# Query normalisation read by ScalarE from the projection's bank, output projection written to the attention output's bank, and weights split in thirds, in a post-norm decoder layer

## The chip, the cores and the metric

The kernel runs on one core of one Trainium2 chip. The metric is the device time of one execution in microseconds (us). Three runs of the kernel before gave 2011.68 us as their median (2011.28 to 2014.92).

## What is computed

A decoder layer on `x` of 4 sequences x 512 rows x 512 columns, in three parts, each followed by a residual sum and a layer norm:

```
x = _layernorm(x + attn(x, Wq, Wk, Wv, Wo))        # attention over the 512 channels
x = _layernorm(x + xattn(x, ctx, ...))             # the part that is changed
x = _layernorm(x + ffn(x, w_gate_up, w_down))      # ternary weights, int8-like activations
```

The middle part, cut to what matters (16 query heads of width 128 in 8 groups, two heads a group; a second set of 16 query heads looks at a context of 64 rows):

```
q  = _ln(fp8_linear(ln_out, wq))     # per head of 128 columns: subtract mean, times rsqrt(var + EPS)
qx = _ln(fp8_linear(ln_out, wqx))
k  = _ln(fp8_linear(ln_out, wk));  v = fp8_linear(ln_out, wv)
kx, vx = split(cond @ w_kv_x);     kx = _ln(kx)
core = softmax(q k^T / sqrt(128)) v;   xout = softmax(qx kx^T / sqrt(128)) vx
out  = round_to_fp8(concat(core, xout) / smooth) @ wproj * scale
```

## The kernel before

**Stages.** Stage A is the first attention, all in fp32. Stage B is the middle part, and the only one whose code changes. Stage C is the feed-forward part. Each engine has its own instruction list, written out by hand, and the engines meet only at counting semaphores: a wait on one engine holds everything that stands behind it on that engine. So the order of the work is exactly the order of the code; there is no planner.

**Loops of stage B.** The outer loop is over 8 groups `g`, the inner one over 4 sequences `b`. One such (g, b) is called a *pair* here, with the number n = 4g + b, 32 in all. A pair has 4 steps `st`, each for 128 rows of queries; a step has the number T = 4n + st. While step `st` of pair n does attention, the engines also project the queries, keys and values of pair n + 1, a tile of 128 rows at a time.

**PSUM banks.** There are 8 banks of 128 x 512 fp32. `S0`, `S1` take the scores of the two heads, `T0`, `T1` the transposed probabilities, `OB` the attention output (columns 0:256 own attention, 256:512 context), `P0` the query projection *and* the output projection, `P1` keys and values, `MB` transposed queries and keys and the context scores.

**A step on TensorE**: two score products (L496), the key/value projection (`proj_kv`) and the query projection (`proj_q`, both through `project`, L391), the attention output `av` of the step before (L446 own, L452 context), the transposes of the probabilities (L530), of the normalised queries (`turn_q`, L425) and, once a pair, of the keys (`turn_k`, L431), and the output projection of two steps before (`project_out`, L458). Step 0 also has the context scores (L567), and in every second pair the context's keys and values (L419); step 1 has the transposes of the context probabilities (L502).

**The path of the queries.** `proj_q` fills `P0`; ScalarE copies it whole to `raw` in SBUF (`raw_kv`, recorded at L662, where all plain copies are) and, behind it, keys and values to `KV`; VectorE takes mean and variance of the four heads from `raw` (`head_stats`, L1017 to L1031); GpSimd computes the inverse deviations in two operations (`deviations`, L1305 and L1307); VectorE normalises keys (`head_norm`, L1039) and the four heads of queries (L1041) into `nq`; TensorE transposes them and ScalarE copies them out with the gain (`qt_out`, L733; `kt_out`, L739, for keys). `P0` is free for the next product as soon as `raw` is written. `turn_k` is the last transposing of a step 3, in the same bank `MB` as `turn_q` just ahead of it, so it waits for `qt_out`.

**The path of the scores.** VectorE takes the row maximum (L1094), ScalarE the exponential with its row sum (L786), VectorE scales the row (`scale_rows`, L1049 and L1051), TensorE transposes, ScalarE copies to `prT` (L662).

**The output.** ScalarE copies `OB` out with the smoothing scale (`ob_out`, L774), VectorE rounds to fp8 in five operations (`round_terms`, L1057 to L1067), TensorE multiplies by `wp` into `P0`, VectorE adds it to `x1` (`accumulate`, L1071). In step T VectorE rounds the terms of T - 1 after it has scaled the rows of T.

**Weights.** A group's four projection matrices arrive in one DMA of 1.5 MB (`load_proj`). Each weight is kept as a sum of two fp16 numbers: ScalarE makes the high part (`split_high`, L700), VectorE the low part (`split_low`, L1010). `wst`, `wh` and `wl` have one buffer each, so the new group's parts are made in the pairs b = 2 and b = 3, after the last use of the old ones and just ahead of the first use of the new ones, which is in step 0 of b = 3.

Of the kernel before, what the change touches and what calls it, by code (L numbers as in the profile page):

```python
# [25 lines left out]
P = 128  # L26
# [15 lines left out]
WCOL = {Q: (0, 256), QX: (256, 512), K: (512, 640), V: (640, 768)}  # L42
NW = 768
# [20 lines left out]
def build(nc, a, out):  # L64
    ctx = ExitStack()
    with ctx:
# [3 lines left out]
        def sb(stack, name, shape, dt=F32):  # L70
# [40 lines left out]
        rdev = sb(ctx, "rdev", [P, 7])  # L111
        mv = sb(ctx, "mv", [P, ST, 2])
# [27 lines left out]
        wst = sb(stB, "wst", [P, KT, NW])  # L140
        wh = sb(stB, "wh", [P, KT, NW], F16)
        wl = sb(stB, "wl", [P, KT, NW], F16)
# [4 lines left out]
        raw = sb(stB, "raw", [P, D])  # L147
# [49 lines left out]
            wst_loaded wkx_loaded wpst_loaded  # L197
# [7 lines left out]
            max_ready exp_done raw_out kv_out kvx_out qt_out kt_out kxt_out ob_out pt_out pxt_out xexp_done  # L205
# [7 lines left out]
        out_stored = [sem(f"out_stored{i}") for i in range(2)]  # L213
        xt_loaded = [sem(f"xt_loaded{i}") for i in range(2)]
# [4 lines left out]
        def tern(c):  # L219
            if c < 8:  # L220
                return wgu[:, c // 2, (c % 2) * F:(c % 2 + 1) * F]
            return wdn[:, (c - 8) * 4:(c - 7) * 4, :].rearrange("p k n -> p (k n)")

# [5 lines left out]
        def _(sp):  # L229
# [21 lines left out]
            def load_proj(g):  # L251
                if g:
                    sp.wait_ge(s["wl_ready"], 4 * g)
                sp.dma_start(wst[:], a["wcat"][g].rearrange("(k p) n -> p k n", p=P)).then_inc(s["wst_loaded"], 16)
# [27 lines left out]
            load_proj(0)  # L282
            load_context(0)
            load_out(0)
# [3 lines left out]
            load_proj(1)  # L288
            for n in range(TT):
# [7 lines left out]
                if b == 3 and g + 2 < NG:  # L297
                    load_proj(g + 2)
                if n + 1 < TT:
                    load_abs(n + 1)  # L300

# [27 lines left out]
        def _(pe):  # L329
# [57 lines left out]
            def project(dst, c, j, b):  # L387
                lo, hi = WCOL[c]
                for k in range(KT):
                    for m, w in enumerate((wh, wl)):  # L390
                        ins = mm(dst, XQ[:, c, k, b * S + j * P:b * S + (j + 1) * P], w[:, k, lo:hi],  # L391
                                 start=(k == 0 and m == 0), stop=(k == KT - 1 and m == 1))
                return ins

            def proj_q(n, j, b, weights=None):
                for c in (Q, QX):
                    lo, hi = WCOL[c]
                    if weights is not None:
                        pe.wait_ge(s["wl_ready"], weights + (3 if c == Q else 4))
                    ins = project(P0[:, lo:hi], c, j, b)  # L400
                ins.then_inc(s["proj_q_made"], 1)

            def proj_kv(n, part, b, weights=None):
                if 3 * n + part:
                    pe.wait_ge(s["kv_out"], 3 * n + part)
                if weights is not None:
                    pe.wait_ge(s["wl_ready"], weights + 2)
                if part == 0:
                    pe.wait_ge(s["kvx_out"], n // 2 + 1)
                    if n >= 2:  # L410
                        pe.wait_ge(s["kxt_out"], (n - 1) // 2 + 1)
                for i, j in enumerate(KVPART[part]):
                    for c, lo in ((K, 0), (V, P)):
                        ins = project(P1[:, 256 * i + lo:256 * i + lo + P], c, j, b)
# [13 lines left out]
            def turn_k(n):  # L428
                pe.wait_ge(s["nq_ready"], 4 * n + 3)
# [4 lines left out]
            def turn_kx(n):  # L434
                pe.wait_ge(s["ident_set"], 2)
                pe.wait_ge(s["nq_ready"], 4 * n + 1)
# [3 lines left out]
            def av(T):  # L440
                n, st = T // ST, T % ST
                pe.wait_ge(s["pt_out"], 2 * T + 2)
                if T:
                    pe.wait_ge(s["ob_out"], T)
                for t in range(ST):
                    mm(OB[:, 0:2 * P], KV[:, n % 2, t, P:2 * P], prT[:, st % 2, t, :, :].rearrange("p h s -> p (h s)"),  # L446
                       start=(t == 0), stop=(t == ST - 1))
                if st == 0:
# [19 lines left out]
            pe.wait_ge(s["wl_ready"], 4)  # L468
            for j in range(4):
                if j:  # L470
                    pe.wait_ge(s["raw_out"], j)
                if j < 3:
                    proj_kv(0, j, 0)
                proj_q(0, j, 0)
# [8 lines left out]
            def pair(g, b, first, last):  # L483
                n = 4 * g + b
                nxt = not (last and b == 3)
                for st in range(ST):
                    T = 4 * n + st
                    if st == 0:
                        pe.wait_ge(s["kt_out"], n + 1)
                        pe.wait_ge(s["qt_out"], 4 * n + 3)  # L490
                    for h in range(2):
                        if T:
                            pe.wait_ge(s["exp_done"], 2 * T + (h - 1))
                        if st == 3 and h == 0:
                            pe.wait_ge(s["qt_out"], 4 * n + 4)
# [8 lines left out]

                    def next_proj():
                        if T >= 3:
                            pe.wait_ge(s["acc_done"], T - 2)
                        if st < 3:
                            proj_kv(n + 1, st, (b + 1) % 4)
                        pe.wait_ge(s["raw_out"], 4 * n + 4 + st)  # L510
                        proj_q(n + 1, st, (b + 1) % 4)

                    if nxt and st in (1, 3):
                        next_proj()
                    if T:
                        av(T - 1)
                    if nxt and st == 2:
                        next_proj()
                    if st == 0 and T >= 2:
                        pe.wait_ge(s["acc_done"], T - 2)  # L520
                        pe.wait_ge(s["raw_out"], 4 * n + 4)
                        project_out(T - 2)
                    for h in range(2):
# [8 lines left out]
                        if h == 0 and st == 0:  # L532
                            pe.wait_ge(s["kt_out"], n + 1)
                            turn_q(n, 3)
                        if h == 0 and st and nxt:
# [871 lines left out]
```

## Time and profile before

| | |
|---|---|
| median of three runs | 2011.68 us |
| the profiled execution, its own time | 2012.47 us |
| its span, first to last instruction | 2010.7 us |
| TensorE busy | 1809.7 us (90%) |
| VectorE busy | 1535.9 us (76%) |
| ScalarE busy | 1064.5 us (53%) |
| GpSimd busy | 263.1 us (13%) |
| mean granted TensorE clock | 0.972 of full |
| chain that ended last | PE 71%, DVE 16%, ACT 9%, issue 3%, POOL 1% |

In the profile PE is TensorE, DVE VectorE, ACT ScalarE, POOL GpSimd, SP the engine that issues DMAs. Busy time of PE goes to the modelled end of its pipelined matmuls, so two matmuls in a row overlap in the records; what a group of matmuls takes of the engine is best read as the distance from its start to the start of the next group. The pairs of stage B lie between 425.6 us and some 1764 us of the span; the start of each pair is seen by the copy of its transposed keys (L739), of which there are 32.

### The profile page before, as it was taken

The numbers are of one execution on the slowest core, as the hardware profiler recorded it, in microseconds if no ns is written. First come the engines' busy times: TensorE is split into PE (matmuls) and PEld (weight loads), VectorE is DVE, ScalarE is ACT, GpSimd is POOL, SyncE is SP. The second block draws the span as 40 slices with busy tenths as digits, with TensorE's granted clock in tenths as the row PEclk, the third lists the DMA queues.
The fourth block names the chain that finished last, engine by engine and source line by source line (L and its number), as shares of the span: only waits on it lengthen the run. The fifth ranks groups of instructions, "written<-read, shape, count | busy, mean of one in ns | idle before, by whom it ended". The sixth has DMA issues, their size and how long they took to land.

```text
span 2010.7 us, 32238 instructions
## 1 busy us (share of the span) xinstructions
PE 1809.7 (90%) x11024; PEld 1248.2 (62%) x11024; DVE 1535.9 (76%) x4964; ACT 1064.5 (53%) x2526; POOL 263.1 (13%) x361
## 2 busy tenths in 40 slices
PE   8999999459999999989999999998999999839897
PEld 3444444337767777777777777777777777614443
DVE  0175754778887888788888788888888888788997
ACT  1121111226666666666666666666666666565555
POOL 0000000011211211111121121111211112011110
PEclk9999999769999999999999999999999999969999
DMA  5000000210011011001101101100110000420000
GB/s 210 21 0 22 0 0 0 75 61 20 17 42 41 10 42 37 21 10 41 42 17 42 42 9 42 37 21 11 39 42 17 10 10 9 176 84 16 22 22 27
DMA packets 37761, 70.78 MB, mean 35 GB/s; under 512 B 3296, under 2 KB 14048, under 8 KB 36576
## 3 DMA queue, kind: packets, MB, share of 16 engines
q1 hardware_dynamic: 37600, 68.73, 10.0%
q8 instruction: 90, 1.47, 0.3%
q14 instruction: 71, 0.58, 0.1%
HBM read 63.47 MB, written 4.19 MB: 34 GB/s over the span
## 4 chain that ended last, share of the span: by engine, by line
PE 71%; DVE 16%; ACT 9%; issue 3%; POOL 1%; DMA 0%; ACTq 0%; POOLq 0%; DVEq 0%; SPq 0%
PE bank L335 17%; PE bank L391 14%; PE bank L446 10%; PE bank L496 10%; PE bank L458 5%; PE bank L530 4%; PE bank L452 3%; PE bank L567 2%; DVE wl L1010 2%; ACT yb L774 2%; PE bank L425 2%; DVE am L1195 2%; ACT qT L733 2%; ACT hb L862 1%; ACT wh L700 1%
## 5 line engine op out<-in xcount | busy, mean ns | idle before, releaser
L391 PE MATMUL bank<-wh,XQ 128*128 128x256 f16 (+1 forms) x2048 | 355.8, 249 | 25.2 <-DVE wl L1010 24.0
L391 PE MATMUL bank<-wl,XQ 128*128 128x256 f16 (+1 forms) x2048 | 359.9, 249 | 0.0
L786 ACT ACTIVATE pr<-bank,nmx 128x512 f32<-128x512 f32 x256 | 175.8, 691 | 178.2 <-DVE nmx L1094 174.5
L496 PE MATMUL bank<-kT,qT 128*128 128x512 f32 x512 | 250.9, 613 | 0.8 <-ACT kT L739 0.7
L446 PE MATMUL bank<-prT,KV 128*128 128x256 f32 x1024 | 242.3, 379 | 0.5 <-ACT prT L662 0.4
L391 PEld LDWEIGHTS bank<-wh,XQ 128*128 128x128 bf16 x2048 | 204.0, 100 | 49.1 <-DVE wl L1010 20.1
L446 PEld LDWEIGHTS bank<-prT,KV 128*128 128x128 f32 x1024 | 189.5, 190 | 52.5 <-issue 23.0
L391 PEld LDWEIGHTS bank<-wl,XQ 128*128 128x128 bf16 x2048 | 202.9, 99 | 22.8 <-issue 10.3
L1307 POOL TENSOR_TENSOR rdev<-gvar,cst 128x7 f32<-128x7 f32 x128 | 190.5, 1488 | 10.0
L1094 DVE TENSOR_REDUCE nmx<-bank 128x1 f32<-128x512 f32 x256 | 169.5, 684 | 25.4 <-PE bank L496 22.1
L774 ACT ACTIVATE yb<-bank,rsT 128x128 bf16<-128x128 f32 x512 | 146.6, 372 | 79.0 <-PE bank L452 79.0
L1305 POOL TENSOR_TENSOR gvar<-mvB,geps 128x7 f32<-128x7 f32 x128 | 27.3, 213 | 1126.2 <-DVE mvB L1031 1126.2
L662 ACT ACTIVATE prT<-bank 128x512 f32<-128x512 f32 x256 | 157.5, 616 | 7.5 <-PE bank L530 7.5
L530 PE MATMUL bank<-identf,pr 128*128 128x128 f32 x1024 | 154.4, 274 | 6.3 <-DVE pr L1051 6.2
L662 ACT ACTIVATE raw<-bank 128x512 f32<-128x512 f32 x128 | 76.3, 596 | 154.4 <-PE bank L391 81.4
L496 PEld LDWEIGHTS bank<-kT,qT 128*128 128x128 f32 x512 | 95.0, 196 | 90.5 <-issue 64.3
L1041 DVE TENSOR_SCALAR nq<-raw,mvB,rdev 128x128 f32<-128x128 f32 x512 | 142.2, 342 | 0.7 <-POOL rdev L1307 0.7
L458 PE MATMUL bank<-wp,cq 128*128 128x512 bf16 x512 | 132.2, 381 | 2.9 <-DVE x L1071 2.9
L733 ACT ACTIVATE qT<-bank,hlq 128x256 f32<-128x256 f32 x256 | 132.7, 584 | 1.2 <-PE bank L425 1.1
L1051 DVE TENSOR_SCALAR pr<-pr,ri 128x512 f32<-128x512 f32 x256 | 124.6, 487 | 9.1
L530 PEld LDWEIGHTS bank<-identf,pr 128*128 128x128 f32 x1024 | 121.6, 142 | 14.7 <-DVE pr L1051 8.3
L614 PE MATMUL bank<-wgu,xiT 128*128 128x512 bf16 x512 | 118.5, 387 | 10.3 <-ACT hs L856 6.9
(157 smaller groups left out, 3032.0 us busy)
## 6 DMA issues: line engine op xcount, KB each, us to landing
wst<-in_wcat SPq DMA_DIRECT2D x8, 1536.0 KB, 6.8
wpst<-in_wproj SPq DMA_DIRECT2D x8, 1024.0 KB, 5.2
wa<-in_wgu SPq DMA_DIRECT2D x32, 256.0 KB, 2.6
wch<-in_wgu SPq DMA_DIRECT2D x8, 1024.0 KB, 12.1
xT<-in_xT SPq DMA_DIRECT2D x4, 1024.0 KB, 5.4
x<-in_x SPq DMA_DIRECT2D x4, 1024.0 KB, 11.9
wkx<-in_wkvx SPq DMA_DIRECT2D x8, 512.0 KB, 4.1
wa<-in_wdn SPq DMA_DIRECT2D x32, 128.0 KB, 2.6
```

Source lines behind the costliest of these rows:

```text
L335: ins = mm(dst, lhs(k), rhs(k), start=(k == 0), stop=(k == n - 1))
L391: ins = mm(dst, XQ[:, c, k, b * S + j * P:b * S + (j + 1) * P], w[:, k, lo:hi], start=(k == 0 and m == 0), stop=(k == KT - 1 and m == 1))
L446: mm(OB[:, 0:2 * P], KV[:, n % 2, t, P:2 * P], prT[:, st % 2, t, :, :].rearrange("p h s -> p (h s)"), start=(t == 0), stop=(t == ST - 1))
L458: ins = mm(P0[:, :], cq[:, T % 2, c * P:(c + 1) * P], wp[:, c, :], start=(c == 0), stop=(c == 3))
L496: mm(SB_[h][:], qT[:, h, st * P:(st + 1) * P], kT[:, :], start=True, stop=True).then_inc(s["scores_made"], 1)
L530: ins = nc.tensor.transpose(TB_[h][:, t * P:(t + 1) * P], pr[:, h, t * P:(t + 1) * P], identf[:])
L662: return act_f(dst, src, ACT.Copy)
L733: ins = act_f(qT[:, 2 * c:2 * c + 2, j * P:(j + 1) * P], MB[:, c * 256:(c + 1) * 256].rearrange("p (h s) -> p h s", h=2), ACT.Identity, sc ...
L774: ins = act_f(yb[:, T % 2, c * P:(c + 1) * P], OB[:, c * P:(c + 1) * P], ACT.Copy, scale=rsT[:, T // 16, c:c + 1])
L786: act_f(pr[:, h, :], SB_[h][:], ACT.Exp, bias=nmx[:, st, h:h + 1], accum_out=su[:, st, h:h + 1]).then_inc(s["exp_done"], 1)
L1094: v.tensor_reduce(nmx[:, st, h:h + 1], SB_[h][:], AX.X, ALU.max, negate=True).then_inc(s["max_ready"], 1)
L1307: g.tensor_tensor(rdev[:], gvar[:], CPOW, ALU.pow).then_inc(s["stats_ready"], 1)
```

## The change

Five things change, all in stage B.

1. **Queries.** `raw` and the copy into it are gone. VectorE's `head_stats` reads `P0` itself. GpSimd's `deviations` has two operations more: the negated means (`nmean`) and their product with the inverse deviations (`nbias`). ScalarE's new `q_norm` writes `nq` straight from `P0` in four activations of 128 x 128 (scale `rdev`, bias `nbias`); it stands at the head of the next step, ahead of the exponentials. VectorE's `head_norm` keeps only the keys, as `k_norm`. TensorE's next `proj_q` waits for `nq_ready`.
2. **Output projection.** It goes to `OB` instead of `P0`: it waits for `ob_out` of the step before, and `av` waits for the `accumulate` before it.
3. **Order.** TensorE: `av_context` is apart from `av` and, in step 1, behind `proj_q`; `turn_k` in step 3 stands ahead of the transposes of the probabilities, and `turn_q(n + 1, 2)` at the end of the step; `project_out` stands at the same place in all steps. VectorE: `round_terms(T - 2)` between the maxima and `scale_rows`, where `round_terms(T - 1)` stood behind; one `accumulate` at the head of each step; `head_stats(n + 1, 0)` ahead of the row sums of the context probabilities. ScalarE follows.
4. **Weights.** They come in thirds of 512 KB (queries; context queries; keys and values) through two slots of `wst`. The query weights have two buffers (`whq`, `wlq`), the key and value weights one. Each third is split in two halves, by ScalarE at the end of steps 2 and 3, by VectorE at the end of step 3 and in step 0 of the next pair, in the pairs b = 0, 1, 2.
5. **DMA queue.** `load_proj` now follows `load_abs` in pairs b = 0, 1, 2, and waits for the split of the third that used the slot.

```diff
-            def raw_kv(n, j, par):
-                act.wait_ge(s["proj_q_made"], 4 * n + j + 1)
-                    act.wait_ge(s["nq_ready"], 4 * n + j)
-                copy(raw[:, :], P0[:, :]).then_inc(s["raw_out"], 1)
+            def q_norm(n, j):
+                act.wait_ge(s["stats_ready"], 4 * n + j + 1)
+                for h in range(4):
+                    ins = act_f(nq[:, j % 2, h * P:(h + 1) * P], P0[:, h * P:(h + 1) * P], ACT.Identity,
+                                scale=rdev[:, h:h + 1], bias=nbias[:, h:h + 1])
+                ins.then_inc(s["nq_ready"], 1)
...
             def head_stats(n, j, par):
-                dve.wait_ge(s["raw_out"], 4 * n + j + 1)
+                dve.wait_ge(s["proj_q_made"], 4 * n + j + 1)
                 for h in range(4):
-                    v.bn_stats(bnB[:, h, :], raw[:, h * P:(h + 1) * P])
+                    v.bn_stats(bnB[:, h, :], P0[:, h * P:(h + 1) * P])
...
-                for h in range(4):
-                    ins = v.tensor_scalar(nq[:, j % 2, h * P:(h + 1) * P], raw[:, h * P:(h + 1) * P], mvB[:, h, 0:1], rdev[:, h:h + 1],
-                                          ALU.subtract, ALU.mult)
-                ins.then_inc(s["nq_ready"], 1)
...
                 own.do(g.tensor_tensor(gvar[:], mvB[:, :, 1], geps[:], ALU.add))
-                own.sync()
-                g.tensor_tensor(rdev[:], gvar[:], CPOW, ALU.pow).then_inc(s["stats_ready"], 1)
+                own.do(g.tensor_tensor(nmean[:], mvB[:, 0:4, 0], cst[:, 5, 0:4], ALU.mult))
+                own.sync()
+                if tile:
+                    pool.wait_ge(s["nq_ready"], tile)
+                own.do(g.tensor_tensor(rdev[:], gvar[:], CPOW, ALU.pow))
+                own.sync()
+                g.tensor_tensor(nbias[:], nmean[:], rdev[:, 0:4], ALU.mult).then_inc(s["stats_ready"], 1)
...
             def project_out(T):
                 pe.wait_ge(s["cq_ready"], T + 1)
+                pe.wait_ge(s["ob_out"], min(T + 2, 4 * TT))
                 for c in range(4):
-                    ins = mm(P0[:, :], cq[:, T % 2, c * P:(c + 1) * P], wp[:, c, :], start=(c == 0), stop=(c == 3))
+                    ins = mm(OB[:, :], cq[:, T % 2, c * P:(c + 1) * P], wp[:, c, :], start=(c == 0), stop=(c == 3))
```

TensorE, a step, after the two score products:

```diff
+                    if nxt and st in (1, 2):
+                        proj_kv(n + 1, st)
...
                     if T:
                         av(T - 1)
+                    if nxt and st == 1:
+                        proj_q(n + 1, st)
+                    if T:
+                        av_context(T - 1)
+                    if nxt and st > 1:
+                        proj_q(n + 1, st)
...
+                    if nxt and st == 3:
+                        pe.wait_ge(s["qt_out"], 4 * n + 4 + 2)
+                        turn_k(n + 1)
...
-                        if h == 1 and st == 3 and nxt:
-                            pe.wait_ge(s["qt_out"], 4 * n + 4 + 3)
-                            turn_k(n + 1)
...
                         project_out(T - 2)
+                    if st == 3 and nxt:
+                        pe.wait_ge(s["kt_out"], n + 2)
+                        turn_q(n + 1, 2)
```

VectorE, a step, after the two maxima:

```diff
+                    if T >= 2:
+                        round_terms(T - 2)
+                    if nxt and st:
+                        k_norm(n + 1, st - 1, (b + 1) % 2)
+                    scale_rows(T, st)
+                    if nxt and st:
+                        head_stats(n + 1, st, (b + 1) % 2)
+                    if b < 3 and not last and st == 3:
+                        split_low(3 * (g + 1) + b, 0)
                     if st == 0:
-                    if T:
-                        round_terms(T - 1)
+                        if b and not last:
+                            split_low(3 * (g + 1) + b - 1, 1)
```

## Rows read from the trace of the kernel before

**Rows 1.** Stretches of pairs b = 0 to 3: stretch, length, busy and records by engine, clock, DMA.
```profile
599.20:639.20 40.00, 38.27 (x282) 30.20 (x280) 33.17 (x117) 26.34 (x67) 6.86 (x8) 1.00 0.11 37
639.20:680.30 41.10, 39.77 (x291) 31.86 (x290) 33.55 (x120) 25.51 (x67) 6.74 (x8) 1.00 0.07 25
680.30:721.20 40.90, 38.23 (x282) 30.22 (x281) 33.16 (x117) 26.68 (x71) 6.87 (x8) 1.00 0.04 11
721.20:766.90 45.70, 41.70 (x291) 32.52 (x290) 38.85 (x136) 28.52 (x75) 7.09 (x9) 0.96 0.14 46
```

**Rows 2.** Waits of PE from 440 to 1720 us: total, times, longest.
```profile
PE bank L431 <- ACT qT L733: 46.4, 30, 2.3
PE bank L391 <- DVE wl L1010: 18.7, 21, 1.8
```

**Rows 3.** Timeline of ACT: starts of pairs n = 1 and n = 31.
```profile
471.37 0.78 ACT L739 ACTIVATE kT<-bank,hln 128x512 f32<-128x512 f32 x1 [0.26 <-PE bank L431]
...
1723.49 0.78 ACT L739 ACTIVATE kT<-bank,hln 128x512 f32<-128x512 f32 x1 [0.26 <-PE bank L431]
```

**Rows 4.** Timeline of PE from a step 3 (b = 1) on: start, length, what, idle before.
```profile
1004.90 1.88 PE L496 MATMUL bank<-kT,qT 128*128 128x512 f32 x4
1006.61 0.27 PE L391 MATMUL bank<-wh,XQ 128*128 128x256 f16 x1
...
1008.36 1.89 PE L446 MATMUL bank<-prT,KV 128*128 128x256 f32 x8
...
1010.53 0.60 PE L530 MATMUL bank<-identf,pr 128*128 128x128 f32 x4
1010.97 0.60 PE L425 MATMUL bank<-identf,nq 128*128 128x128 f32 x4
...
1013.33 0.66 PE L431 MATMUL bank<-identf,kn 128*128 128x128 f32 x4 [1.32 <-ACT qT L733]
1013.82 1.03 PE L458 MATMUL bank<-wp,cq 128*128 128x512 bf16 x4
1014.86 1.98 PE L496 MATMUL bank<-kT,qT 128*128 128x512 f32 x4
...
1027.76 0.66 PE L502 MATMUL bank<-identf,px 128*128 128x128 f32 x4 [0.39 <-DVE px L1125]
```

**Rows 5.** Timeline of DVE around the same place, in steps 3 and 0.
```profile
1009.89 0.86 DVE L1017 BATCH_NORM_STATS2 bnB<-raw 128x6 f32<-128x128 f32 x4
...
1017.49 1.11 DVE L1041 TENSOR_SCALAR nq<-raw,mvB,rdev 128x128 f32<-128x128 f32 x4
1018.51 0.16 DVE L1049 RECIPROCAL ri<-su 128x1 f32<-128x1 f32 x1
...
1020.22 0.29 DVE L1057 TENSOR_SCALAR yb<-yb 128x512 bf16<-128x512 bf16 x1 [0.44 <-ACT yb L774]
...
1022.01 0.75 DVE L1071 SCALAR_TENSOR_TENSOR x<-bank,pscale,x 128x512 f32<-128x512 f32 x1
```

**Rows 6.** Timeline of POOL, the same tile.
```profile
1011.25 0.20 POOL L1305 TENSOR_TENSOR gvar<-mvB,geps 128x7 f32<-128x7 f32 x1 [4.31 <-DVE mvB L1031]
1011.54 1.48 POOL L1307 TENSOR_TENSOR rdev<-gvar,cst 128x7 f32<-128x7 f32 x1
```

**Rows 7.** Timeline of ACT, steps 2 to 0 of the same pairs.
```profile
1005.43 0.50 ACT L743 ACTIVATE kxT<-bank,hln 128x128 f32<-128x128 f32 x1
...
1008.88 0.60 ACT L662 ACTIVATE raw<-bank 128x512 f32<-128x512 f32 x1 [0.56 <-DVE nq L1041]
1010.74 1.14 ACT L774 ACTIVATE yb<-bank,rsT 128x128 bf16<-128x128 f32 x4 [1.26 <-PE bank L452]
...
1016.75 0.69 ACT L786 ACTIVATE pr<-bank,nmx 128x512 f32<-128x512 f32 x1 [1.94 <-DVE nmx L1094]
```

**Rows 8.** Groups of stage B by line: busy, mean ns | idle before.
```profile
L1094 DVE TENSOR_REDUCE nmx<-bank 128x1 f32<-128x512 f32 x206 | 136.5, 684 | 20.8 <-PE bank L496 18.0
...
L1121 DVE TENSOR_REDUCE su<-px 128x8 f32<-128x512 f32 x26 | 17.8, 685 | 13.2 <-ACT px L823 13.2
L1022 DVE BATCH_NORM_STATS2 bnB<-KV 128x6 f32<-128x128 f32 x104 | 26.6, 278 | 0.0
```

**Rows 9.** DMA issues: KB each, median us to landing.
```profile
wkx<-in_wkvx SPq DMA_DIRECT2D x8, 512.0 KB, 4.1
```

More of the change, by code:

```diff
@@ L204, in build @@
             xs_made pxt_made out_made
-            max_ready exp_done raw_out kv_out kvx_out qt_out kt_out kxt_out ob_out pt_out pxt_out xexp_done
+            max_ready exp_done kn_ready kv_out kvx_out qt_out kt_out kxt_out ob_out pt_out pxt_out xexp_done
             bn_ready stats_ready nq_ready pr_scaled xs_sub px_scaled cq_ready acc_done
@@ L213, in build @@
         out_stored = [sem(f"out_stored{i}") for i in range(2)]
+        wst_loaded = [sem(f"wst_loaded{i}") for i in range(2)]
         xt_loaded = [sem(f"xt_loaded{i}") for i in range(2)]
@@ L532, in pair @@
                         if h == 0 and st == 0:
-                            pe.wait_ge(s["kt_out"], n + 1)
+                            pe.wait_ge(s["qt_out"], 4 * n + 3)
                             turn_q(n, 3)
-                        if h == 0 and st and nxt:
+                        if h == 0 and st in (1, 2) and nxt:
                             if st == 1:
@@ L691, in _, with split_high @@
             x_out(NB - 1)
-            def split_high(g, parts):
-                act.wait_ge(s["wst_loaded"], 16 * g + 16)
-                for c in parts:
-                    lo, hi = WCOL[c]
-                    for k in range(KT):
-                        ins = act_f(wh[:, k, lo:hi], wst[:, k, lo:hi], ACT.Copy, scale=srel[:, c, k:k + 1])
-                    ins.then_inc(s["wh_ready"], 1)
+            def split_high(part, ks):
+                act.wait_ge(wst_loaded[part % 2], 16 * (part // 2) + 16)
+                for c in WPART[part % 3]:
+                    for k in ks:
+                        ins = act_f(split_weights(part // 3, c, k)[0], staged(part, c, k), ACT.Copy, scale=srel[:, c, k:k + 1])
+                ins.then_inc(s["wh_ready"], 1)
             def rows_proj(g):
@@ L748, in _ @@
             act.wait_ge(s["insc_ready"], 1)
-            split_high(0, (K, V, Q, QX))
+            for part in range(3):
+                split_high(part, (0, 1))
+                split_high(part, (2, 3))
             act.wait_ge(s["vx_cleared"], 1)
@@ L752, in _ @@
             for j in range(4):
-                raw_kv(0, j, 0)
+                if j < 3:
+                    kv_copy(0, j)
+                    q_norm(0, j)
                 if j:
@@ L816, in pair @@
                         rows_proj(g)
-                    if st == 0 and b == 3 and not last:
-                        split_high(g + 1, (QX,))
+                    if b < 3 and not last and st in (2, 3):
+                        split_high(3 * (g + 1) + b, (0, 1) if st == 2 else (2, 3))
                     if st == 0:
@@ L824, in pair @@
                         if nxt:
-                            raw_kv(n + 1, 0, (b + 1) % 2)
-                    if st == 3 and b == 2 and not last:
-                        split_high(g + 1, (Q,))
+                            kv_copy(n + 1, 0)
             for b in range(NB):
@@ L1077, in _ @@
             own.sync()
-            split_low(0, (K, V, Q, QX))
+            for part in range(3):
+                split_low(part, 0)
+                split_low(part, 1)
             for j in range(4):
@@ L1117, in pair @@
                                         ALU.subtract).then_inc(s["xs_sub"], 1)
-                        if b == 3 and not last:
-                            split_low(g + 1, (QX,))
+                        if nxt:
+                            head_stats(n + 1, 0, (b + 1) % 2)
                         dve.wait_ge(s["xexp_done"], n + 1)
```

232 lines of the change are left out of this document (106 added, 126 removed).

## Prediction

> **What bounds the kernel now.** I read the page first (busy shares and the slices of the span): TensorE is busy 90% of the span at a clock of 0.972, VectorE 76%, and the slices are flat through stage B, which is some two thirds of the time. So the question is how much of stage B TensorE stands still, and why. Three views answer it, in this order.
>
> The stretches of single pairs [rows 1]: pairs b = 0 to 3 take 40.0, 41.1, 40.9 and 45.7 us, 167.7 a group. TensorE is busy 38.3, 39.8, 38.2 of the first three; the fourth has the same work as the second (291 matmuls in each) and takes 4.6 more, at a clock of 0.96. VectorE has 33.2 of 40.0 and ScalarE 26.3. TensorE is near its limit, VectorE next.
>
> The waits of TensorE in the same region [rows 2]: 46.4 us in 30 waits of `turn_k` on ScalarE's `qt_out`, up to 2.3 each, and 18.7 us on the weights' low parts, which fall on the boundaries of groups.
>
> The timeline of a step 3 [rows 4]: the transposes of h1 start at about 1011.41 and take 0.44 (1010.53 to 1010.97 is the distance for one such group), and `turn_k` starts at 1013.33: 1.5 us lost. What stands behind it costs a little more each time: the scores of the next pair start at 1014.86, 0.2 after the output projection's four (0.87) are through, since they wait for the new kT, and in even pairs the context transposes lose 0.5 (0.39 and the drained pipeline). Taking these off 40.0 and 41.1, a pair of pure TensorE work is 37.7 us (b even) or 39.5 (b odd, with the context's keys and values). A group has 154.4 of work in 167.7. All that any order can give in the 30 pairs from n = 1 to n = 30, which last from 471.4 to 1723.5, 1252.1 us [rows 3], is 1252.1 - 15 x (37.7 + 39.5) = 94 us.
>
> **What each part costs or gives.** Times below are after the start of the score products of a step.
>
> *TensorE's prices* [rows 4]: scores 1.71, a tile of queries 1.75, of keys and values half of that in columns, 0.89, `av` with its context part 2.17 (of it 0.44 context), each group of four transposes 0.44, `project_out` 0.87 (1013.82 to 1014.69, the 0.17 to 1014.86 being the wait). No instruction is added or removed; only waits change.
>
> *turn_k.* Ahead of the h0 transposes it no longer stands behind a `turn_q` of its own step. It needs keys of the step before and `qt_out(n + 1, 1)`, a step old. The 46.4 us go. `turn_q(n + 1, 2)` takes its place at the end and needs `kt_out`, issued at `turn_k`'s end (6.1 of the step); `project_out` only ends at 7.8, and ScalarE's copy (0.78 [rows 3]) behind `ob_out` is done by 7.1. Nothing late.
>
> *Weights.* The halves are made one pair or more ahead for queries. For keys and values (one buffer) the last half is made by VectorE in step 0 of b = 3 behind `scale_rows`, at 6.5, and first needed behind kvx and the context scores, at 9.6. The 18.7 us of waits and the slow clock behind them (45.7 against 41.1 is 4.6 a boundary, seven boundaries, 32 us in all with `turn_k`'s share) go. ScalarE's and VectorE's work on weights is the same, spread over three pairs: 0.8 to 1.1 at each of six places on ScalarE, 0.8 on VectorE. DMAs: three of 512 KB for one of 1536 KB, each asked for about a pair before use, where one of that size lands in 4.1 [rows 9]; `load_abs` ahead of them in the queue is released in step 2, in time for the next step 2. Cost 0 in the loop.
>
> *VectorE.* It loses the four normalisations, 1.02 a tile (1017.49 to 1018.51 [rows 5]), 4.1 a pair: 33.2 to about 29. The rounding (1020.22 to 1022.01, 1.79) moves between maxima and scaling. That is time in which VectorE waited for the exponentials, but not all of it: maxima end at 2.6, rounding at 4.4, the keys' normalisation at up to 5.0; then h0 is scaled 0.7 later.
>
> *ScalarE.* `raw` (0.6, some 0.5 of the engine's time) goes, `q_norm` comes: four of 128 x 128. The nearest rows are `ob_out`, four such copies with a scale in 1.14, and `kxT`, one with scale and bias by pointer, 0.50, so at most 2.0 for four [rows 7]. It is the same function with the same operands as `kxT`, but such activations overlap (as those of `ob_out` do: 1.14 for four of 0.37), so I take 1.55, and keep 1.14 and 2.0. Net 2.6 to 6.0 more a pair, I take 4.2: 26.3 to 30.5 of 38, no bound by load.
>
> *GpSimd.* Two operations of the kind of `gvar`, 0.20 and its 0.08 to 0.09 hand-over [rows 6]: the path from statistics to `stats_ready` grows from 1.8 to 2.3.
>
> **Where waits come instead.** Three chains must fit into TensorE's order.
>
> (a) The scaled row h0. In steps 2 and 3 TensorE needs it at 6.5 and 6.1 and has it at 5.7 and 5.2. In step 0 with b even it needs it at 1.71 + 2.17 + 0.89 = 4.8 and has it at 5.0 to 5.1: 0.3 lost. With b odd kvx (eight records of 256 columns, as `av`'s 1.73) takes the place of the 0.89: nothing lost. In step 1 VectorE is late, because `head_stats(n + 1, 0)` stands ahead of the context's row sums: it waits for the product that TensorE makes last in step 0, then for ScalarE's copy of the keys behind the context exponential, so `px` is scaled 3.4 (b even) to 3.7 (b odd) into step 1, where TensorE is at its transposes at 3.5. Then `accumulate` (0.66) must be through before `av`: 0.2 to 0.3 lost; the rows, rounding and keys behind it cost 0.2 more at h0. Together 0.4 (even), 0.5 (odd).
>
> (b) The round trip of `P0`: statistics 1.36 (1009.89 to 1011.25 [rows 5, 6]), up to 0.4 more with keys, GpSimd 2.3, `q_norm` 1.55: 5.2 to 5.6. TensorE has between two query products 5.7 (step 0 to 1), 7.4 (1 to 2), 6.1 (2 to 3) and over 10 (3 to 0). At 2 to 3 ScalarE's sums and its part of the split stand ahead of `q_norm`: 0.1 lost with b even, 0.3 with b odd. Behind `q_norm` stand the exponentials: exp h0 starts at 3.3 to 3.8 instead of 1.9 (1016.75 after 1014.86 [rows 7, 4]), which the rounding and `k_norm` cover; without this cover it would cost 1.4 to 1.9 at each of four steps.
>
> (c) The cycle of `OB`: `ob_out` 1.14, `project_out` 0.87, `accumulate` 0.75, and back to `av` after 1.71 of scores. It is released before TensorE needs it in steps 0, 2, 3; in step 1 the context part is late by the query product (ends at 8.0) and `project_out` at 9.2 touches it: 0.1.
>
> So a pair is 37.7 + 0.3 + 0.4 + 0.1 = 38.5 (even), 39.5 + 0.5 + 0.3 + 0.1 = 40.4, which I round up to 40.6 for the step behind the loading of `wp`. Thirty pairs: 15 x (38.5 + 40.6) = 1186.5, that is 65.6 less.
>
> *Given back outside.* At the start, the third third waits for the first to be split and then for its DMA (4.1 [rows 9]): the splits end 2.5 later, on VectorE's path; three tiles save 1.0 and lose 0.5 on it, -1.6; the first exponentials stand behind `q_norm`, +1.6; pair 0 saves 1.5 of its stalls: +1. In the last pair nothing fills TensorE, so the rounding ahead of the scaling is on the path in three steps (0.5 to 1.3 each), and at the end `project_out(LT - 2)` and its `accumulate` (0.87 + 0.75 and hand-overs) no longer overlap the last `ob_out`: +5 together.
>
> Sum: 2012.5 (the profiled execution's own time, its span of 2010.7 and 1.8 around it) - 65.6 + 1 + 5 = 1952.9. That execution is 0.8 over the median, so 1952.
>
> **A price that rows do not settle.** The statistics now read a bank. A reduction of 512 takes 0.684 from a bank and 0.685 from SBUF [rows 8], so I take 0 more; the dearest row of 128 wide is a normalisation's, about 0.34 (1.11 for four that start 0.25 apart [rows 5]) against 0.278 for the statistics [rows 8], so at most 0.065 each, 0.26 a trip.
> The Trainium skill, "VectorE: DVE Perf Modes", section on the TRN2 errata, gives 120 cycles fixed for a PSUM source and 58 for SBUF at 0.96 GHz, an estimate of 0.065 us for each of the four; its "Rules for kernel authors" says to copy to SBUF first "if you'll do many ops", which speaks against the first edit: eight reads of `P0` where one was. By that the time would be that of the second rival below; the reduction's rows do not show such a difference.
>
> **Rivals.**
> 1. *The round trip of `P0` decides* (hand-overs that I priced at a tenth and queueing on VectorE and ScalarE add 0.5 to each trip). Its two tight places, 0 to 1 and 2 to 3, stall by 0.4 each: 0.8 x 31 = 25, giving 1977. For: slack is 0.1 to 0.5 there, and VectorE's list is in order. Against: all prices come from rows, and prices of hand-overs are in them.
> 2. *Reading the bank is dearer*, 0.26 a trip: 0.5 a pair, 16 us, 1968.
> 3. *No new stall*: the 94 us all come, less 6 outside: 1924. Against: in steps 0 and 1 VectorE's chain ends after TensorE's on my own count.
> 4. *Slower than before*: `q_norm` ahead of the exponentials in ScalarE's queue makes every late statistic a late row. The trip covers itself up to about 0.15; beyond it each tenth costs two places, and h0 as well from 1.0 on. The 60 us are gone when the trip is 1.1 longer than counted (6.5 instead of 5.4); at 1.4 longer, the three places take 1.25 + 1.25 + 0.4 = 2.9 a pair, 90 us, 2042. For: it is one serial loop over four engines. Against: it would need GpSimd or ScalarE at twice their rows.
> 5. *The parts do less than they say*: only the boundaries are mended (18.7 and the clock, 7 x 4.6 = 32) and `turn_k`'s wait returns at `turn_q(n + 1, 2)`: 2012 - 32 + 6 = 1986.
>
> **Chances and range.** Forecast 0.45 (its own range 1940 to 1962), rivals 0.22, 0.11, 0.08, 0.08 and 0.06. A measurement of this kernel tells 0.2% (4 us) from no change. Faster: all but rival 4, 0.92, less 0.04 for outcomes between rivals 5 and 4 that land within 0.2%: 0.88, 0.04, and 0.08 slower. Leaving out most of rival 3 and all of rival 4, the range is 1930 to 1990.
>
> **What would show it.** After: the rows of L431 <- `qt_out` and L391 <- `wl` gone from TensorE's waits in the loop; pair lengths 38.5 and 40.6 with no long b = 3 and the clock at 1.00 there; VectorE near 29 a pair and ScalarE near 30; `q_norm`'s four in 1.55 (1.14 to 2.0), statistics from `P0` at 0.278 (to 0.343) each; TensorE's new waits on `pr` and `px` (steps 0, 1) of tenths. I am wrong if TensorE waits for `nq` or for `accumulate` by more than 0.5 a time, if a pair is over 40 (even), or if start and end cost more than 10.

## The result, and the profile after

| | before | after |
|---|---|---|
| median | 2011.48 us | 1949.45 us (1949.14 to 1949.86) |
| span of the profiled execution | 2010.7 | 1947.6 |
| TensorE busy | 1809.7 (90%) | 1808.5 (93%) |
| VectorE busy | 1535.9 (76%) | 1413.8 (73%) |
| ScalarE busy | 1064.5 (53%) | 1159.9 (60%) |
| GpSimd busy | 263.1 (13%) | 311.4 (16%) |

The ratio is 0.9688, 95% interval [0.9671, 0.9705]: 62 us faster. The forecast was 1952 us and a ratio of 0.970. One execution each of e1_turnk and e5_start, the profiled one, ran throughout at a far lower granted clock; their times below leave it out, and no row of it is shown.

The same stretches as in [rows 1], pairs b = 0 to 3, in the changed kernel (stretch, length, busy and records of PE, PEld, DVE, ACT, POOL, clock, DMA share, GB/s), and behind them the last pair with its end:

```profile
593.44:631.78 38.34, 38.23 (x282) 30.18 (x281) 29.39 (x103) 30.19 (x81) 8.32 (x17) 1.00 0.12 39
631.78:671.98 40.20, 40.10 (x291) 31.80 (x290) 31.39 (x110) 29.84 (x83) 8.55 (x16) 1.00 0.13 39
671.98:710.51 38.53, 38.40 (x282) 30.17 (x281) 30.89 (x107) 29.17 (x80) 8.55 (x16) 1.00 0.08 25
710.51:750.63 40.12, 40.02 (x291) 31.79 (x290) 31.90 (x114) 29.52 (x82) 8.28 (x16) 1.00 0.09 26
1655.30:1699.90 44.60, 34.01 (x158) 22.67 (x156) 27.14 (x69) 21.61 (x58) 1.71 (x4) 0.93 0.43 182
```

A group takes 157.2 where it took 167.7; the long fourth pair and its lowered clock are gone. The seven largest waits of TensorE's matmuls over the whole span (total, times, longest):

```profile
PE bank L411 <- ACT nq L720: 26.1, 3, 9.2
PE bank L608 <- ACT xib L859: 21.1, 2, 11.6
PE bank L642 <- ACT hT L671: 16.5, 16, 1.2
PE bank L364 <- DVE xn L980: 13.9, 1, 13.9
PE bank L355 <- DMA Wq<-in_Wq: 8.8, 1, 8.8
PE bank L411 <- DVE wlk L1019: 8.6, 1, 8.6
PE bank L554 <- DVE pr L1057: 7.5, 4, 4.5
```

None of these lies in the loop: asked for 476 to 1650 us alone, the view gives no wait of the matmuls at all, where [rows 2] had 65 us. (`nq` 3 times, `wlk` once and the longest of `pr` are the start of stage B, the other three of `pr` the last pair; the rest are stages A and C.) The engine's weight loads, which the view counts apart, still wait a little there, and these are what is left of the waits on other engines:

```profile
PEld bank L579 <- ACT qT L740: 10.7, 30, 0.4
PEld bank L554 <- DVE pr L1057: 4.0, 15, 0.3
PEld bank L411 <- ACT nq L720: 1.5, 7, 0.2
```

The price rows that the forecast had bounded came out like this, as count and minimum, median and maximum in ns:

```profile
L720 ACT ACTIVATE nq<-bank,nbias,rdev x512: 444/458/525, 396.7 to 1657.6; 128x128 f32<-128x128 f32 x171
```
```profile
L1026 DVE BATCH_NORM_STATS2 bnB<-bank x512: 279/281/302, 392.6 to 1653.5; 128x6 f32<-128x128 f32 x171
```

The third row is the same statistics in the kernel before, read from `raw` in SBUF:

```profile
L1017 DVE BATCH_NORM_STATS2 bnB<-raw x512: 273/277/297, 388.4 to 1719.9; 128x6 f32<-128x128 f32 x171
```

Four marks split the 63.1 us by which the spans differ: the first score product of pair 1, that of the last pair, the start of the last addition to `x1`, and the end. The first of them (before, after):

```profile
472.20 1.98 PE L496 MATMUL bank<-kT,qT 128*128 128x512 f32 x4
```
```profile
476.57 1.88 PE L519 MATMUL bank<-kT,qT 128*128 128x512 f32 x4
```

| | before | after | difference |
|---|---|---|---|
| to pair 1 | 472.20 | 476.57 | +4.4 |
| pairs 1 to 30 | 1252.1 | 1178.7 | -73.4 |
| last pair, to the last addition | 38.6 | 44.6 | +6.0 |
| stage C | 247.7 | 247.7 | 0 |

### The profile page after: what moved, and what is told of

Same layout as the page of the kernel before. It is cut to its first block, busy times and chain, and to the rows that moved or that the text cites. A ratio compares the mean times of both kernels' runs of the same rounds, so it can differ in the third digit from the quotient of the medians.

```text
span 1947.6 us, 32324 instructions
## 1 busy us (share of the span) xinstructions
PE 1808.5 (93%) x11024; PEld 1247.4 (64%) x11024; DVE 1413.8 (73%) x4452; ACT 1159.9 (60%) x2910; POOL 311.4 (16%) x618
## 3 DMA queue, kind: packets, MB, share of 16 engines
q1 hardware_dynamic: 46048, 68.73, 10.9%
## 4 chain that ended last, share of the span: by engine, by line
PE 80%; DVE 10%; ACT 4%; issue 4%; POOL 1%; DMA 1%; POOLq 0%; DVEq 0%; ACTq 0%; SPq 0%
PE bank L355 17%; PE bank L411 16%; PE bank L519 11%; PE bank L469 10%; PE bank L485 6%; PE bank L554 6%; PE bank L579 3%; PE bank L446 3%; PE bank L478 3%; DVE am L1198 2%; PE bank L440 1%; ACT hb L871 1%; PE bank L623 1%; DVE hh L1193 1%; ACT hs L865 1%
## 5 line engine op out<-in xcount | busy, mean ns | idle before, releaser
L720 ACT ACTIVATE nq<-bank,nbias,rdev 128x128 f32<-128x128 f32 x512 | 193.1, 463 | 185.7 <-POOL nbias L1315 184.9
L411 PE MATMUL bank<-whq,XQ 128*128 128x256 f16 x1024 | 237.4, 278 | 26.3 <-ACT nq L720 26.1
L469 PE MATMUL bank<-prT,KV 128*128 128x256 f32 x1024 | 247.3, 385 | 2.5 <-DVE x L1077 0.9
L519 PE MATMUL bank<-kT,qT 128*128 128x512 f32 x512 | 241.7, 594 | 0.8 <-ACT kT L746 0.8
L411 PE MATMUL bank<-wlq,XQ 128*128 128x256 f16 x1024 | 237.2, 277 | 0.0
L469 PEld LDWEIGHTS bank<-prT,KV 128*128 128x128 f32 x1024 | 190.1, 191 | 60.2 <-issue 40.1
L671 ACT ACTIVATE prT<-bank 128x512 f32<-128x512 f32 x256 | 151.5, 605 | 34.1 <-PE bank L554 33.4
L1026 DVE BATCH_NORM_STATS2 bnB<-bank 128x6 f32<-128x128 f32 x512 | 113.9, 285 | 44.9 <-PE bank L411 44.8
L1077 DVE SCALAR_TENSOR_TENSOR x<-bank,pscale,x 128x512 f32<-128x512 f32 x128 | 95.9, 749 | 52.9 <-PE bank L485 51.6
L411 PE MATMUL bank<-whk,XQ 128*128 128x128 f16 x1024 | 125.8, 220 | 8.6 <-DVE wlk L1019 8.6
L411 PEld LDWEIGHTS bank<-whq,XQ 128*128 128x128 bf16 x1024 | 103.0, 101 | 41.5 <-ACT nq L720 28.4
L623 PE MATMUL bank<-wgu,xiT 128*128 128x512 bf16 x512 | 118.4, 386 | 10.4 <-ACT hs L865 6.9
```

What stands on the lines that cost most here:

```text
L671: return act_f(dst, src, ACT.Copy)
L720: ins = act_f(nq[:, j % 2, h * P:(h + 1) * P], P0[:, h * P:(h + 1) * P], ACT.Identity, scale=rdev[:, h:h + 1], bias=nbias[:, h:h + 1])
```

## Experiments

Each experiment is a variant of the kernel before or of the changed kernel. Theory 1 is that of the prediction: what was gained is TensorE's waits taken away, and the rest of the change had to fit around it. Theory 2: it is VectorE's load, 142 us of normalisations less, that made the difference. The diffs below are cut to the lines that matter.

### e1_turnk: only the keys' transposes moved, in the kernel before

```diff
+                    if nxt and st == 3:
+                        pe.wait_ge(s["qt_out"], 4 * n + 4 + 2)
+                        turn_k(n + 1)
...
-                        if h == 1 and st == 3 and nxt:
-                            pe.wait_ge(s["qt_out"], 4 * n + 4 + 3)
-                            turn_k(n + 1)
...
+                    if st == 3 and nxt:
+                        pe.wait_ge(s["kt_out"], n + 2)
+                        turn_q(n + 1, 2)
```

> The kernel before with one thing of the change: in step 3 the keys are transposed ahead of the probabilities, and turn_q(n + 1, 2) behind the output projection; weights and the path of the queries are as before. Theory 1 (the gain is TensorE's waits taken away, and they do not come back elsewhere): each pair loses its 1.5 us wait and the 0.2 at the next scores, b = 2 some 2.4, of which about 0.9 comes back because the split of keys and values delays the copy of kT; 31 pairs x 1.6 = 50 us, 1962 us. Theory 2 (what made the change faster is VectorE's load, 142 us of normalisations less; with that load in place a wait removed returns as another): 1995 us or more.

Measured: 1953.74 us, ratio 0.9705 [0.9689, 0.9721] to the kernel before (2012.46 beside it), in three executions from 1951.8 to 1955.1. That is 59 us, 9 more than theory 1 said and far from theory 2. Moving two groups of four transposes, and ScalarE's copies of them, with VectorE's load untouched, gives nearly as much as the whole change (59 of 62). Where the 9 us come from stays open.

### e2_split: only the weights in thirds and a pair ahead

```diff
+                    if b < 3 and not last and st in (2, 3):
+                        split_high(3 * (g + 1) + b, (0, 1) if st == 2 else (2, 3))
...
+                if b < 3 and 3 * (g + 1) + b + 2 < 3 * NG:
+                    load_proj(3 * (g + 1) + b + 2)
```

> The kernel before with the weights in thirds, split a pair ahead, and nothing else of the change. Theory 1: the seven boundary pairs go from 45.7 to about 41.1 (-32), the eight pairs b = 2 lose the 0.9 that the split of keys and values added to turn_k's wait (-8), the start costs 2.5 more: 1974 us, and all pairs between 40.0 and 41.1. Theory 2: the same work of ScalarE and VectorE spread over steps that are full already: each pair b = 0 to 2 grows by 0.5 to 1, 1990 us or more.

Measured: 1978.88 us, ratio 0.9833 [0.9818, 0.9847], 33.6 less. All pairs take 39.9 or 41.1 now, none grew. Its waits of `turn_k` remain (480 to 1640 us):

```profile
PE bank L449 <- ACT qT L748: 36.9, 28, 1.3
PE bank L519 <- DVE px L1140: 5.5, 14, 0.4
```

Theory 1 said 1974, so its size was 5 us too large and its kind right; theory 2's growth of 0.5 to 1 a pair is not there. By the marks the 30 pairs give 37.1 and the start takes 2.6 back. Thirds of a transfer and an earlier split were not tried apart.

### e3_both: these two together, nothing else of the change

> The kernel before with both: the keys transposed earlier and the weights split ahead; queries still go through raw and VectorE, the output projection through P0. Theory 1: the two gains add up, pairs of 38.3 (b even) and 39.5 (b odd): 30 pairs 1167 against 1252, start +2.5, nothing at the end: 1930 us, which is less than the changed kernel, so that the edits of the query path and of the output's bank would have brought nothing by themselves. Theory 2 (VectorE's load decides): 1960 us or more, at least 10 over the changed kernel.

Measured: 1931.63 us, ratio 0.9598 [0.9584, 0.9613]. The interval lies wholly under that of the changed kernel: 18 us faster than it, with queries still copied to `raw` and normalised by VectorE, and the output projection still in `P0`. The four pairs of a group:

```profile
590.36:628.49 38.13, 37.74 (x283) 30.24 (x282) 32.98 (x117) 26.68 (x70) 7.21 (x10) 1.00 0.12 39
628.49:668.00 39.51, 39.47 (x292) 31.78 (x291) 34.75 (x124) 26.55 (x71) 6.72 (x9) 1.00 0.13 39
668.00:706.37 38.37, 37.95 (x283) 30.16 (x282) 34.36 (x121) 25.75 (x69) 6.85 (x9) 1.00 0.09 26
706.37:746.15 39.78, 39.48 (x292) 31.74 (x291) 35.28 (x128) 26.26 (x71) 6.72 (x9) 1.00 0.09 26
```

VectorE has 33 to 35 us in a pair here against 29 to 32 in the changed kernel, and the pairs are shorter. Theory 2 falls. By the same marks as above, of the 18.1 us between the two spans (1929.5 and 1947.6) the 30 pairs hold 10.8 (1167.9 against 1178.7), the start 2.5, the last pair 5.7, and stage C gives 0.9 back. Theory 1 had said 1930 us.

### e4_raw: the changed kernel, queries by their old path

```diff
+            def raw_copy(n, j):
+                act.wait_ge(s["proj_q_made"], 4 * n + j + 1)
+                if 4 * n + j:
+                    act.wait_ge(s["nq_ready"], 4 * n + j)
+                copy(raw[:, :], P0[:, :]).then_inc(s["raw_out"], 1)
```

> The changed kernel with the path of the queries as before: ScalarE copies P0 to raw behind ob_out, VectorE takes the statistics from raw and normalises the four heads behind k_norm and ahead of scale_rows; order, banks and weights as changed. By the working of the prediction the scaled row comes 1.0 us later in each step: with slack of 0.8 in steps 2 and 3, none in step 0 (b even) and step 1: about 2.1 us a pair more, less the 0.2 of the shorter trip of P0: 60 us more than the changed kernel, 2010 us. If VectorE's order leaves room and the query path does not matter: 1949 within 5.

Measured: 2031.84 us, ratio 1.0102 [1.0085, 1.012]: 82 us over the changed kernel where 60 were expected, and 19 slower than the kernel before. Pairs are 41.3 and 42.6, which is 2.7 more each, not 1.9. The waits are where the working had put them, on the scaled row and on `px` (480 to 1640 us):

```profile
PE bank L555 <- DVE pr L1061: 39.8, 56, 1.1
PE bank L528 <- DVE px L1135: 15.3, 28, 0.6
```

So in the *changed order*, with the rounding between the maxima and the scaling, ScalarE's normalisation is worth 82 us; in the *order before*, e3_both does without it. The edits of the query path and of VectorE's order go together, and neither is needed for the gain. The output projection's move to `OB` was never run by itself, so what it costs or gives is not known.

### e5_start and e6_px: is there more in e3_both

```diff
             for part in range(3):
+                if part == 2:
+                    quant_x(NB - 1, 0, (0, 1))
                 split_low(part, 0)
                 split_low(part, 1)
```

> The kernel of e3_both with one edit at the start of stage B: VectorE does two of the sixteen roundings of the last sequence's rows (4.6 us) while the third third of the weights is on its way, where it stood still for 4.0 us in the changed kernel. If that DMA's wait is on the path (VectorE's list is the path of the start): 3.5 to 4 us less, 1928. If TensorE's first product, which comes no earlier, is what counts: 0 to +1.

Measured: 1929.5 us, ratio 0.9581 [0.9565, 0.9597]; that overlaps e3_both's interval: 2 us that this measurement can't tell from none. In the trace of e6_px, which has this edit too, the first transposed keys are copied at 426.5 (428.9 in e3_both), but pair 0 then takes 46.0 (43.8), so pair 1 starts at the same time. The granted clock takes the 2.4 us back: over pair 0 it is 0.78 of full in e6_px and 0.88 in e3_both, and the whole loss lies in step 0 of that pair (20.1 against 17.3 between score products), where the sixteen matmuls of the context scores run at the lower level of 1.2 GHz. Ahead of this stretch TensorE had stood 6.2 us (e3_both) and 5.9 us (e6_px) for the first scaled row. The context scores in either:

```profile
443.46 1.95 PE L585 MATMUL bank<-kxT,qT 128*128 128x64 f32 x16
```
```profile
441.41 3.62 PE L587 MATMUL bank<-kxT,qT 128*128 128x64 f32 x16
```

In the changed kernel the clock over pair 0 is 0.88 with this edit (e10_ends) and without it, and there pair 1 starts 4.4 earlier: the DMA's wait was on the path of the start. Why the clock rose later in e6_px is not known.

```diff
+                    if nxt and st == 1:
+                        proj_kv(n + 1, st)
                     if st == 1:
                         pe.wait_ge(s["px_scaled"], n + 1)
```

> e5_start and, in step 1, the keys and values projected ahead of the context transposes, as in the changed kernel. In e3_both TensorE waits 0.4 to 0.5 for px in the pairs with b even (15 waits, 5.8 us), the last wait of any size there. If nothing else is late, 5 to 7 us less than e5_start: 1922. If the late copy of the context probabilities then holds the context part or the transposes of h0: the same as e5_start within 2.

Measured: 1919.7 us, ratio 0.9537 [0.9523, 0.9551], 10 under e5_start, where 5 to 7 were expected, and 30 under the changed kernel: the fastest of all. Against e3_both the loop gives 8.7 (pairs 1 to 30 in 1159.2 instead of 1167.9). The waits of `px` in the view sum to 5.8, but step 1 with b even goes from 10.64 to 10.04, so 0.6 was lost at each. The pairs with b even are 37.53 and 37.79, and one wait of the matmuls is left in the loop:

```profile
589.64:627.17 37.53, 37.37 (x280) 30.27 (x282) 32.68 (x117) 26.69 (x69) 7.07 (x10) 1.00 0.12 40
627.17:666.70 39.53, 39.33 (x289) 31.75 (x291) 34.76 (x124) 26.61 (x71) 6.77 (x9) 1.00 0.13 39
```
```profile
PE bank L551 <- DVE pr L1071: 2.1, 7, 0.3
```

That is the 37.7 and 39.5 of pure TensorE work that the prediction had read from the kernel before, within 0.3. By this view little is left to gain in the loop by order alone; no run here tries to go below it.

### e7_trip2 and e8_trip5: the round trip of P0 made longer

In the changed kernel, twice here and five times in e8_trip5:

```diff
+                for _ in range(2):
+                    own.do(g.tensor_tensor(nbias[:], nmean[:], rdev[:, 0:4], ALU.mult))
+                    own.sync()
                 g.tensor_tensor(nbias[:], nmean[:], rdev[:, 0:4], ALU.mult).then_inc(s["stats_ready"], 1)
```

> The changed kernel with two more products of nbias (0.28 each with its hand-over, 0.56 together) on GpSimd ahead of stats_ready, so that the trip of P0 is 0.56 longer and no other engine has more work. By the rule of rival 4 in the prediction (slack 0.15, two tight places): 0.8 a pair, +25 us. By the trace of the changed kernel: at 2 to 3 ScalarE's sums and split end 0.6 after the statistics in b = 0 to 2, so the longer trip hides there, and costs 0.3 at 0 to 1: +12 us.

> The same with five more (1.4 us). By the rule of rival 4: 1.25 + 1.25 + 0.4 = 2.9 a pair, +90 us, slower than the kernel before by 25. By the trace of the changed kernel: 0.8 to 1.2 at 2 to 3, 1.1 at 0 to 1: 2.0 a pair, +62 us, about level with the kernel before. If the trip does not bind: +0.

Measured: 1963.48 us (0.9752 [0.9737, 0.9767]), +14, and 2043.06 us (1.0147 [1.013, 1.0164]), +94. The first is near the 12 that the trace of the changed kernel said, half of what the rule of rival 4 said; the second is near the rule's 90, not the trace's 62. By the marks the 30 pairs take 12.1 and 85.4 more, 0.40 and 2.85 a pair (the rule had 0.8 and 2.9), and the start 2.5 and 8.9. So part of the longer trip is hidden. Where, the loop of the changed kernel suggests: ScalarE has a wait for `nbias` at only 55 of its some 120 normalisations there, and at the others it comes about when the statistics are ready, or later:

```profile
ACT nq L720 <- POOL nbias L1315: 143.6, 55, 4.3
```

With 1.4 us more, TensorE itself waits for `nq` at 55 places and for the scaled row at 14, which fits that everything behind `q_norm` on ScalarE moves too. The waits of e8_trip5 (480 to 1640 us):

```profile
PE bank L411 <- ACT nq L720: 47.1, 55, 1.1
PE bank L554 <- DVE pr L1057: 11.0, 14, 1.0
```

Rival 4 was a real way to fail: the gain of 62 us is gone somewhere between 0.56 and 1.4 us of longer trip. The prediction had said 1.1.

### e9_roundback: the rounding behind scale_rows

```diff
-                    if T >= 2:
-                        round_terms(T - 2)
                     if nxt and st:
                         k_norm(n + 1, st - 1, (b + 1) % 2)
                     scale_rows(T, st)
+                    if T >= 2:
+                        round_terms(T - 2)
```

> The changed kernel with the rounding of the terms of T - 2 behind scale_rows again, where VectorE does not wait, and nothing else moved. By its trace: in steps 2 and 3 the row is scaled no earlier, because the exponentials stand behind q_norm and are what scaling waits for; so the rounding (1.8) delays the statistics (up to 1.8), the terms for project_out (0.3 to 0.8 a step) and the next accumulate: about 3.5 a pair, +100 us, 2050. If only the place of scale_rows counted, it would gain 0.3 a pair at step 0 and 1940 would come.

Measured: 2045.45 us, ratio 1.0164 [1.0148, 1.0179], +96. Expected +100, and the waits are on the rounded terms:

```profile
PE bank L485 <- DVE cq L1073: 58.6, 82, 1.2
PE bank L485 <- ACT qT L740: 17.2, 27, 0.7
PE bank L411 <- ACT nq L720: 9.8, 27, 0.4
```

With `q_norm` ahead of the exponentials, the rows come late, and of the two places tried for the rounding the changed kernel's is better by 96 us. In the order before, e3_both rounds behind the scaling at no such cost.

### e10_ends: the changed kernel's start and end mended

```diff
-                        round_terms(T - 2)
+                        if nxt:
+                            round_terms(T - 2)
...
                     scale_rows(T, st)
+                    if not nxt:
+                        round_terms(T - 2)
...
+                if T == 4 * TT - 2:
+                    pe.wait_ge(s["nq_ready"], 4 * TT)
+                    dst = P0
```

> The changed kernel with three edits outside the loop: VectorE rounds two parts of the last rows while the third third of the weights lands (as in e5_start: -2 to -4); in the last pair the rounding stands behind scale_rows (-2 to -3); the last output projection but one goes to P0 and overlaps ob_out (-1.5 to -1.9). If start and end are what the prediction mis-sized (about 10 us where it had 6), 6 to 8 us less than the changed kernel: 1942. If the end is bound elsewhere: under 3.

Measured: 1945.48 us, ratio 0.9667 [0.9651, 0.9683], 4 under the changed kernel with overlapping intervals, between the 6 to 8 and the "under 3" of the two cases expected. In its trace pair 1 starts 4.4 us earlier and the part behind the loop is 2.0 shorter (44.6 from the last copy of the keys to the last addition, against 46.6), 1.0 of which stage C gives back. The start is mended to the value of the kernel before (472.1 against 472.2); of the 6.0 at the end only a third is, and by which of its two edits this run does not tell.

## Why the prediction was right, step by step

- **What bounds the kernel**: right. TensorE's 37.7 and 39.5 a pair, taken from waits and gaps of the kernel before, are borne out by e6_px (37.5 to 37.8 and 39.5 to 39.8).
- **turn_k**: right that the wait goes and does not return. Alone it is worth 59 us (e1_turnk), where its wait of 1.5 a pair and the 0.2 at the next scores gave 50.
- **Weights**: right. 33.6 alone (e2_split), in its trace 37.1 in the loop less 2.6 at the start; 32 was the term for the loop. The two overlap by 59 + 34 - 81 = 12. Part of it can be seen: e2_split also shortens the pairs b = 2, from 40.9 to 39.9, which had been longer than the pairs b = 0 in step 3, where `turn_k` waits (10.9 against 10.0). The rest is not shown: no row of e1_turnk is there to show it.
- **Queries**: prices right. `q_norm`'s four take 1.50 (forecast 1.55, bounds 1.14 to 2.0), a pair of ScalarE 29 to 30 (forecast 30.5). A pair of VectorE is 29.4 to 31.9, forecast 29: the forecast left out that the low parts of the weights, which had stood in one pair (38.85 against 33.2 in [rows 1]), are now spread over three.
- **Chains (a), (b), (c)**: 38.3 to 38.5 a pair against 38.5, and 40.1 to 40.2 against 40.6; the loop gave 73.4 where 65.6 stood. No wait of the matmuls shows these losses, but the distances between score products do. Medians in us, b even / b odd; "bare" is e6_px, and for step 0 with b odd the kernel before:

| step | bare | changed | more | forecast |
|---|---|---|---|---|
| 0 | 10.54 / 12.27 | 10.88 / 12.29 | 0.3 / 0 | 0.3 / 0 |
| 1 | 10.04 / 10.04 | 10.46 / 10.72 | 0.4 / 0.7 | 0.5 / 0.6 |
| 2 | 8.70 / 8.81 | 8.76 / 8.87 | 0.1 / 0.1 | 0 / 0 |
| 3 | 8.25 / 8.25 | 8.24 to 8.44 / 8.24 to 8.32 | 0 to 0.2 / 0 to 0.1 | 0.1 / 0.3 |

  The terms stand where they were put. Of the 7.8 that the loop gave beyond the forecast, 3 are the 0.2 rounded up in the odd pairs for the loading of `wp`, which costs nothing that can be seen (and lies in b = 0, an even pair), and most of the rest is the 0.3 of step 3 with b odd, of which 0 to 0.1 is there.
- **Start and end**: sized too small, +10.4 against +6. The start is +4.4 where +1 stood. The splits end 4.2 later instead of 2.5, the wait for the third third's DMA being whole on the chain that ended last:

```profile
375.63 4.21 DMA wst<-in_wcat
```

  The three tiles save 1.7 (1.6 forecast) and the late exponentials cost 1.7 (1.6 forecast). Behind the first scaled rows pair 0 saves nothing where 1.5 stood, and the rows show a term that the prediction left at nothing, the clock. TensorE, which had stood 5.9 us for the first row before and 4.5 after, is granted the higher level (2.4 GHz) for good from 439 us on in the kernel before; in the changed one it has the lower level (1.2 GHz) from 441 to 451. Its context scores there take 1.79 to the next product before and 3.47 after. The stretches behind the first scaled rows (before, after):

```profile
436.60:472.20 35.60, 33.78 (x256) 27.36 (x254) 25.95 (x100) 21.87 (x54) 6.87 (x8) 0.96 0.19 70
```
```profile
440.90:476.57 35.67, 35.41 (x237) 28.44 (x236) 22.62 (x85) 23.34 (x62) 7.06 (x15) 0.86 0.10 35
```

  The end is +6.0 against +5. The three steps in which the rounding stands on the path wait 0.98 to 0.99 for the scaled row, within the 0.5 to 1.3 forecast; again some of it is the clock, which falls to the lower level for 3.4 us in step 1, where `av` takes 3.03 to the next group against 2.08 in the kernel before. Why the clock goes as it does at these two places is not tested. The misses of the ends and the loop's nearly cancel (4.4 more, 7.8 less), so the total (1949 against 1952) is better than its terms: that part is luck.
- **Rival 2**, statistics dearer from a bank: wrong. The median is 281 ns from the bank against 277 from `raw`. The Trainium skill's table in "VectorE: DVE Perf Modes" (TRN2 errata section) has 120 cycles fixed for a PSUM source and 58 for SBUF at 0.96 GHz, which makes the difference 65 ns, an estimate. The 4 ns measured here do not agree with it, and the measurement decides.
- **Where the reading misled**: the prediction named the query path and the output's bank as parts that cost little and let the reader take them as parts of the gain. They are not. With the keys' earlier transposes and the early weights alone the time is 1931.6 (e3_both). What the rest costs in the loop, 0.2 to 0.7 a pair, is in the prediction's own chains (a) to (c), which come from the query path, from `OB` and from VectorE's order; it did not ask what the change would be without its first two edits and most of the third.

## What to carry to other kernels

When one engine is nearly full, list its waits and price each edit by the wait that it removes. Here the normalisations taken from VectorE removed none, and the kernel that kept them was the faster one. A change made of many edits should be priced with each left out, since edits may only repair what others broke: here 82 us of one edit's value existed only in the order that another had made. A loop over several in-order engines has slack in the queue of each: here 0.56 us more on a round trip cost 0.4 a pair, and 1.4 us cost 2.85. And where the fullest engine stands still for some us, look at its granted clock behind the pause as well as at the pause.

## What the runs showed of the hardware

VectorE's statistics over 128 columns cost nearly the same from a PSUM bank (281 ns, median of 512) as from SBUF (277 ns). ScalarE's activation of 128 x 128 with scale and bias by pointer, written as fp32, takes 458 ns in its record and about 0.35 us from start to start in a row of four (1.50 in all), where in the kernel before a copy with a scale pointer, written as bf16, takes 0.37 and 1.14. The sixteen matmuls of the context scores take 1.79 us to the next product at the granted level of 2.4 GHz (kernel before, pair 0) and 3.47 at 1.2 GHz (changed kernel, the same place).
